# Moving one of the four probability copies of the first attention loop from VectorE to ScalarE, between its exponentials

## The reference

```python
x = x + jnp.tanh(g_xattn[0]) * _L0_xattn_ref(_layernorm(x), ctx, ctx, mask, w_q, w_k, w_v, w_o)
x = x + jnp.tanh(g_ffn[0]) * _L0_ffn_ref(_layernorm(x), gate_w, gate_b, w1, w2, w3, ws1, ws2, ws3)
# the second layer: attention with a bias per query and key, then experts of another kind

def _L0_xattn_ref(q, k, v, mask, w_q, w_k, w_v, w_o):      # 16 heads of 8
    qh, kh, vh = split(q @ w_q.T), split(k @ w_k.T), split(v @ w_v.T)
    scores = jnp.einsum('bhqd,bhkd->bhqk', qh, kh) / jnp.sqrt(8.0)
    attn = jax.nn.softmax(jnp.where(mask, scores, NEG), axis=-1)
    out = jnp.einsum('bhqk,bhkd->bhqd', attn, vh)
    return out.transpose(0, 2, 1, 3).reshape(...) @ w_o.T
# _L0_ffn_ref: softmax of x @ gate_w.T, the best 6 of 64 experts of each token, their MLPs
```

## Time and profile before

| | us |
|---|---|
| median of 3 runs | 1015.98 |
| lowest and highest | 1013.45, 1022.74 |
| the profiled execution | 1013.34 |
| its span, first to last instruction | 1011.5 |

### The profile page before, as it was taken

One profiled execution on the slowest core, in us unless ns is written; L12 is line 12 of the kernel. 1 busy time (PEld: TensorE's weight loads), 2 busy tenths in 40 slices (PEclk: granted clock), 3 DMA queues, 4 the chain that ended last, 5 costly groups with the idle time before them and its releaser, 6 DMA issues. The chain is left out here.

```text
span 1011.5 us, 30714 instructions
## 1 busy us (share of the span) xinstructions
PE 787.9 (78%) x9969; PEld 586.2 (58%) x9969; DVE 742.1 (73%) x2256; ACT 497.3 (49%) x1719; POOL 551.9 (55%) x950
## 2 busy tenths in 40 slices
PE   1999999999956998089999999999960249888780
PEld 1677777777743766057677676776740126755560
DVE  2789999999986664158888888888869774676334
ACT  1677777777741221046676766767640014333220
POOL 2576444444323675476776766767510065777772
PEclk9999999999987999579999999999985559999995
DMA  5111211121213342233333423324210122666658
GB/s 147 57 67 69 76 69 69 68 72 70 85 44 99 97 117 76 58 103 111 108 115 110 132 94 126 120 99 132 78 39 0 31 66 67 185 188 185 167 154 238
DMA packets 98744, 100.84 MB, mean 100 GB/s; under 512 B 24511, under 2 KB 76077, under 8 KB 98659
## 3 DMA queue, kind: packets, MB, share of 16 engines
q1 hardware_dynamic: 92002, 90.09, 28.6%
q0 software_dynamic: 6656, 9.66, 3.4%
HBM read 60.84 MB, written 44.17 MB: 104 GB/s over the span
## 5 line engine op out<-in xcount | busy, mean ns | idle before, releaser
L543 ACT ACTIVATE P<-bank,mx 128x120 f32<-128x120 f32 x1024 | 276.5, 425 | 42.9 <-DVE mx L780 42.7
L448 PE MATMUL bank<-ident,P 128*120 128x128 f32 x1024 | 166.1, 285 | 32.4 <-ACT P L543 30.8
L780 DVE TENSOR_REDUCE mx<-bank 128x4 f32<-128x480 f32 x256 | 149.6, 646 | 6.4 <-PE bank L435 4.1
L448 PEld LDWEIGHTS bank<-ident,P 128*120 128x120 f32 x1024 | 107.6, 138 | 77.1 <-ACT P L543 42.1
L607 POOL TENSOR_SCALAR rs<-mv 128x1 f32<-128x1 f32 x128 | 28.9, 226 | 174.2 <-DVE mv L762 174.1
L464 PE MATMUL bank<-PT,Vb 120*32 120x128 f32 x2048 | 105.9, 279 | 0.0
L1582 POOL DMA_INDIRECT xg<-token_rows,tokens x64 | 66.3, 1036 | 71.2 <-DVE tokens L1636 49.6
L464 PE MATMUL bank<-PT,headcols 120*32 120x128 f32 x2048 | 102.8, 273 | 0.0
L425 PE MATMUL bank<-bp,identb 128*128 128x480 bf16 x384 | 101.3, 375 | 1.2 <-POOL bp L626 1.2
L634 POOL TENSOR_TENSOR Qm<-qf,qmask 128x512 f32<-128x512 f32 x64 | 66.6, 1040 | 65.4 <-ACT qf L527 63.7
L1592 POOL DMA_INDIRECT expert_sums<-y,sum_rows x64 | 71.5, 1118 | 26.8 <-issue 18.6
(11 more groups left out here) (239 smaller groups left out, 1797.0 us busy)
## 6 DMA issues: line engine op xcount, KB each, us to landing
expert_sums<-zeros SPq DMA_DIRECT2D x32, 512.0 KB, 3.5
choice_rows<-zeros SPq DMA_DIRECT2D x32, 384.0 KB, 2.4
yrows<-choice_rows SPq DMA_DIRECT2D x32, 384.0 KB, 3.1
XT<-expert_sums SPq DMA_DIRECT2D x16, 512.0 KB, 6.8
XS<-expert_sums SPq DMA_DIRECT2D x16, 512.0 KB, 6.6
w<-in_w13T SPq DMA_DIRECT2D x8, 704.0 KB, 4.3
token_rows<-payload SPq DMA_DIRECT2D x32, 128.0 KB, 1.7
ctx<-in_ctxT SPq DMA_DIRECT2D x64, 60.0 KB, 2.1
```

The lines of the kernel that those rows point to most:

```text
L448: mm = nc.tensor.transpose(TB[r % 2][0:KV, S * j:S * j + S], t.P[:, r, j, :], t.ident[:])
L543: e = nc.scalar.activation(t.P[:, r, j, :], heads(SC[r])[:, j, :], ACT.Exp, bias=t.mx[:, G * r + j:G * r + j + 1], scale=-1.0)
L780: ve.tensor_reduce(t.mx[:, G * r:G * r + G], heads(SC[r]), AX.X, ALU.min).then_inc(ev.mins, 1)
```

## The change

In the first attention block the copy of the turned group 1 goes from VectorE to ScalarE. VectorE copies group 0 alone; ScalarE copies 1, 2 and 3. On ScalarE the copy of group 1 stands behind `router_exp` and ahead of the exponentials of groups 2 and 3. The semaphores' counts follow: `pt_act` counts three a batch instead of two, `pt_dve` one. TensorE's matmuls and their order stay as they are, and so does the second attention block.

```diff
             def turn(b, r):
 
                 pe.wait_ge(ev.exped, G * b + r + 1)
-                if r < 2:
+                if L == 0 and r == 0:
+                    used(pe, ev.pt_act, 3 * (b - 1) + 2)
+                elif L == 0 and r == 1:
+                    used(pe, ev.pt_act, 3 * b)
+                elif L == 0 and r == 2:
+                    pe.wait_ge(ev.pt_dve, b + 1)
+                elif L == 0:
+                    pe.wait_ge(ev.pt_act, 3 * b + 1)
+                elif r < 2:
                     used(pe, ev.pt_act, 2 * (b - 1) + r + 1)
                 else:
                     pe.wait_ge(ev.pt_dve, 2 * b + r - 1)
...
             def values(b, v, r):
 
 
-                if r < 2:
+                if L == 0 and r == 0:
+                    pe.wait_ge(ev.pt_dve, b + 1)
+                elif L == 0:
+                    pe.wait_ge(ev.pt_act, 3 * b + r)
+                elif r < 2:
                     pe.wait_ge(ev.pt_dve, 2 * b + r + 1)
                 else:
                     pe.wait_ge(ev.pt_act, 2 * b + r - 1)
...
                 if on(i, -4) is not None:
                     router_exp(on(i, -4), u)
+                if L == 0 and here is not None:
+                    keep_turned(here, 1)
                 if here is not None:
                     exponentials(here, 2)
                     exponentials(here, 3)
...
                 if L == 0 and s1 is not None:
                     normalise(before, w, s1)
-                if here is not None:
+                if L == 1 and here is not None:
                     keep_turned(here, 1)
                 if s4 is not None:
                     router_invert(on(i, -4), u, s4)
```

## The result

| | kernel before | changed kernel |
|---|---|---|
| median | 1014.72 us (4 runs) | 1037.70 us (4 runs, 1036.63 to 1038.75) |
| ratio, 95% interval | 1 | 1.0216 (1.0152 to 1.0279) |
| profiled execution | 1013.34 us, span 1011.5 | 1038.75 us, span 1037.0 |

The change makes the kernel slower by some 23 us.

The account below looks back on a forecast made before the run. VectorE, 93% busy in the first attention loop, was taken to end last in each step. The terms 12.0, 6.4, 3.1 and 1.0 gave +22.5 us, 1035.8, or 1038.5 by the median; 1037 was taken, range 1025 to 1047.

Parts of the forecast that it names:

- the wait: On ScalarE, the copy waits for group 1 turned, until 0.69 after its transposition, holding back the exponentials of groups 2 and 3.
- The chain: First attention loop, scores to next scores through TensorE's turning, ScalarE's copy and exponentials: 8.90 to 9.15 us, taken as 9.0.
- the side branch of group 3: End of the chain: group 3's exponentials, last mask and scores take 2.65 against 2.57 through group 2, could add 0.08 us.
- Steps 8 to 27: The loop's twenty steps: 9.0 us each in place of 8.40, together 12.0 us more.
- Steps 0 to 7: Start of the first attention block: 63.64 us before, 70.0 with the change, 6.4 us more.
- Steps 28 to 30: Three steps after the loop: 23.89 us before, 27.0 with the change, 3.1 us more.
- Step 31: Last step of the first block: the exponentials of groups 2 and 3 begin 1.0 us later.
- The small delays at VectorE's rounds would be hidden too: In the loop: VectorE's delays at each round, in the 8.40 us mean step before, would add nothing to the changed step.
- the residual's branch: Scores through VectorE's residual and `head_min` to turning group 0: 3.81 us against TensorE's 3.96, just hidden; otherwise 0.2 a step.
- VectorE still sets the pace: Rival, end of VectorE's step: each step takes VectorE's 7.69 us, 17 us less in all, 996 us; chance 0.08.
- It cancels: Rival, in each step: relieving VectorE starts everything 0.6 to 1.2 us earlier, offsetting the wait; 1011 to 1018 us; chance 0.10.
- The clock: Rival, on TensorE: lower busy share drops the clock to 1.2 GHz for some steps, about 1060 us; chance 0.04.

Follow-up runs that it names:

- copy_behind: The changed kernel with ScalarE's copy of group 1 moved behind the exponentials of groups 2 and 3; 0.9953 of the kernel before, 246.6 us for the 31 steps.
- dve_refilled: The changed kernel with VectorE adding zeros where its copy of group 1 stood; 1.0297 of the kernel before, 278.7 us for the 31 steps.
- behind_refilled: copy_behind with VectorE adding zeros where its copy of group 1 stood; 1.0020 of the kernel before, 256.2 us for the 31 steps.
- copy_alone: The kernel before with a spare ScalarE copy of zeros ahead of group 2's exponentials, without a wait; 1.0079 of the kernel before, 263.1 us for the 31 steps.
- spare_behind: The kernel before with a spare ScalarE copy of zeros behind the exponentials of groups 2 and 3; 1.0012 of the kernel before, 255.5 us for the 31 steps.

## Why the prediction was right

**The direction and the size.** 1037 forecast, 1037.7 measured. That they agree to 0.7 us is in part luck: the sum gave 22.5 us, the medians differ by 23.0, the two profiled executions by 25.5, and the kernel before alone varied by 12 us over its four runs. The step that carried it was the wait: ScalarE's copy starts 0.69 behind TensorE's transposition (0.69 in the trace after), and the exponentials of groups 2 and 3 queue behind it. copy_behind shows it by the same work with the wait elsewhere. The rule of the Trainium skill that ScalarE's queue is strictly first in, first out (PSUM — Partial Sum Buffer, Engine vs sequencer instructions) fits this: no exponential passed the waiting copy.

**The chain.** Predicted 8.90 to 9.15, I took 9.0. The plain steps take 8.98 from scores to scores. Turning group 2 waits 1.27 to 1.35 where I said 1.3 to 1.6, and comes 2.34 behind group 1 in plain steps and 2.42 in the others, where I said 2.4. The exponentials' piece was 1.16 in plain steps, at the lower of my two values (1.23 in the others), and the piece from group 2 to the scores 1.32 in place of 1.23: there the side branch of group 3 comes through, for which I had allowed 0.08.

**The sum, term by term.** Steps 8 to 27: +12.0 forecast, 13.1 measured. Steps 0 to 7: +6.4, 7.0 (70.65 against 63.64). Steps 28 to 30: +3.1, 2.7. Step 31: +1.0; from its `head_min` to the next block's first matmul 23.66 against 22.39, +1.3. Together 24.1 where I had 22.5. The span grew by 25.5; the start was 0.3 earlier, and 1.7 lie in blocks that the change doesn't touch. I have no cause for these.

**Where a step failed.** "The small delays at VectorE's rounds would be hidden too": they were not. One step of each round takes 9.27 from scores to scores, and 9.05 is the mean; the 0.05 over my 9.0 makes the missing 1.1 us of the loop. There VectorE's `head_min` has 0.23 of issue (time in which the engine waited for nothing that the profile shows), and group 0's exponentials come too late for TensorE:

```profile
207.00 2.35 DVE L794 TENSOR_REDUCE mx<-bank 128x4 f32<-128x480 f32 x4 [0.23 <-issue]
```

```profile
208.94 0.65 PE L456 MATMUL bank<-ident,P 128*120 128x128 f32 x4 [0.23 <-ACT P L555]
```

So the residual's branch, which I counted as just hidden, comes through in one step of four, and "no idle time before group 0's transposition" holds in the other three. I had sized that branch at 3.81 from scores to group 0, with 0.45 from the projection to the residual. The residual comes 0.53 behind the projection, `head_min` 2.09 behind the scores (213.96 to 216.05), and group 0 could be turned 1.17 behind its exponentials of 216.72: 3.93, which is 0.03 short of TensorE's 3.96 and leaves no room for the 0.23. And the idle time ahead of the copy is 0.31 to 0.43, not 0.5 or more. My 0.51 ran from start to start, while the bracket counts from the end of the row before: in the kernel before that row, the router's read of its sum, started at 204.10 and took 0.29, which leaves 0.31 to 204.70.

**VectorE.** Its waits came where I said, at the copy of group 0 (0.16 to 0.26, in three steps of four) and the residual (1.0), its busy share is 80%. dve_refilled shows that its relief is worth at most 0.4 us in the changed kernel.

**The rivals.** "VectorE still sets the pace" needed a chain of 7.7 and promised 17 us. The changed kernel's chain was 8.98, and with the wait out of the way copy_behind got 8.9 us: the ring 0.29 behind VectorE takes the rest. The rule of the Trainium skill to optimise the engine of the highest occupancy first (Perfetto Trace Analysis, Identifying the Most-Contended Engine) named the right engine here: by behind_refilled all of that gain is VectorE's relief. "It cancels" had a flaw that I did not see: it spoke of 1.2 us of lateness on VectorE as slack. copy_alone shows that ScalarE's slack there is under 0.3, since what is late is not only the scores but the projection. The clock did not fall: 1.00 from 200 to 250 us, as before.

## What to carry to other kernels

Before a copy is moved to an engine with time to spare, ask what it waits for there and what is queued behind it. In an engine that works in order, a wait ahead of work that others need joins their chains into one ring; add up that ring from the rows, starts to starts, and compare it with the step. Here the same copy cost 23 us ahead of eight exponentials and gained 9 behind them.

The slack of an engine is not the time by which its input comes early. It is the distance from the present step to the next ring, and a spare instruction put in that place measures it in one run: 0.52 us added and 0.26 a step lost leave 0.26, against 0.29 by the rows.

## What the hardware showed that I had not expected

The kernel before took 1014.6 us in one session and 1084.8 and 1082.0 us in two others. It was profiled in the first alone, but the changed kernel and copy_behind have the same 31 steps in the first and the third session, to 0.2 us. The windows of the kernel before, from its first profile:

```profile
0.00:300.00 300.00, 252.73 (x4098) 197.71 (x4098) 253.48 (x799) 205.46 (x801) 133.40 (x303) 0.99 0.22 75
300.00:450.00 150.00, 102.06 (x774) 70.11 (x773) 74.20 (x245) 28.67 (x62) 87.62 (x111) 0.83 0.31 90
```

And those of spare_behind, whose 31 steps equal it, from the second session:

```profile
0.00:300.00 300.00, 252.72 (x4098) 197.56 (x4098) 253.71 (x800) 221.94 (x833) 133.06 (x303) 0.99 0.22 75
300.00:450.00 150.00, 101.16 (x658) 68.19 (x658) 62.41 (x222) 20.07 (x35) 65.81 (x67) 0.80 0.23 67
```

In the first 300 us TensorE's 4098 matmuls and their time agree. In the expert block behind them it is 658 matmuls in place of 774, and 67 GB/s in place of 90. The granted clock is 0.80 in place of 0.83 there. So a difference starts in the expert block, which gathers and scatters rows by DMA. Whether the transfers are its cause is not shown, nor which of them it would be. The results name chip 5 both for 1014.6 and for 1082.0 us, and chip 0 for 1084.8, so the number of the chip does not tell the sessions apart. Times of a whole kernel from two sessions can't be compared here; the stretches of the loop can.
